# Big 128-column products split into side-by-side pairs of 64 columns in a three-layer graph network on one core

## The reference, cut to what matters

```python
N, E, D, L = 12500, 400000, 64, 3          # nodes, edges, width, layers; dst is sorted
h = relu(layernorm(x))
for l in range(3):
    def mlp(z): return relu(z @ W1[l] + b1[l]) @ W2[l] + b2[l]
    agg = segment_sum(mlp(h[dst]), src, N)  # row = src, col = dst
    h = mlp(h + agg)
out = x + h @ Wf + bf
```

## Time and profile before

| | |
|---|---|
| median of 3 runs | 2153.08 us (2151.14 to 2156.22) |
| the profiled execution | 2150.84 us, of which the span of the trace is 2149.1 us |
| PE busy in the span | 1983.8 us |
| DVE busy | 1443.7 us |
| ACT busy | 840.0 us |
| POOL busy | 598.2 us |
| mean granted TensorE clock | 0.977 |

### The profile page before, as it was taken

How to read it: one execution, slowest core, us unless ns; L and a number is a source line. 1 busy time by engine, 2 the same in 40 slices (tenths; PEclk the granted TensorE clock), 3 DMA queues, 4 the chain that set the end, 5 groups by cost and what they waited for, 6 DMA issues and landing times.

```text
span 2149.1 us, 42352 instructions
## 1 busy us (share of the span) xinstructions
PE 1983.8 (92%) x16959; PEld 1077.5 (50%) x16959; DVE 1443.7 (67%) x1656; ACT 840.0 (39%) x2196; POOL 598.2 (28%) x273
## 2 busy tenths in 40 slices
PE   4565889999999999999999999999999999999998
PEld 3454545555555555544455455455445555555554
DVE  7999999999999999946643343343465444444343
ACT  4896988888888888822200000000010000000000
POOL 3666666666666666600000000000000000000000
PEclk9786999999999999999999999999999999999999
DMA  7356666666666666653444543543544555545452
GB/s 201 73 138 184 176 183 203 200 196 195 192 194 192 193 192 189 187 180 91 151 150 121 164 149 105 171 144 118 164 150 123 171 167 155 161 151 166 137 164 71
DMA packets 332835, 344.60 MB, mean 160 GB/s; under 512 B 21562, under 2 KB 303992, under 8 KB 332184
## 3 DMA queue, kind: packets, MB, share of 16 engines
q1 hardware_dynamic: 327516, 335.59, 53.2%
q0 software_dynamic: 2352, 6.43, 1.1%
q10 hardware_dynamic: 2816, 0.53, 0.2%
HBM read 252.58 MB, written 89.89 MB: 159 GB/s over the span
## 4 chain that ended last, share of the span: by engine, by line
PE 61%; DVE 24%; issue 6%; DMA 4%; POOL 2%; SPq 1%; ACT 1%; DVEq 0%; POOLq 0%
PE ps L1546 49%; DVE arena L756 13%; PE ps L1411 7%; DVE arena L764 5%; DMA arena<-counts_dram 4%; POOL arena L638 2%; PE ps L1496 2%; DVE arena L804 2%; DVE arena L796 2%; PE ps L1378 1%; PE ps L1523 1%; SPq L455 1%; PE ps L1406 1%; DVE arena L729 1%; DMA counts_dram<-arena 1%
## 5 line engine op out<-in xcount | busy, mean ns | idle before, releaser
L1546 PE MATMUL ps<-arena,parts 128*128 128x448 fp8e4 x5488 | 1049.4, 353 | 1.4 <-DVE arena L892 1.4
L1546 PEld LDWEIGHTS ps<-arena,parts 128*128 128x128 f16 x5488 | 531.6, 98 | 518.4 <-issue 27.1
L879 DVE TENSOR_SCALAR arena<-arena 128x3136 uint16<-128x3136 uint16 x196 | 191.3, 976 | 586.8 <-PE ps L1546 586.8
L638 POOL TENSOR_TENSOR arena<-arena,weight_now 128x416 int32<-128x416 int32 x196 | 507.1, 2587 | 279.9 <-DVE arena L756 275.9
L1411 PE MATMUL ps<-arena,parts 128*128 128x448 fp8e4 x2744 | 554.2, 354 | 1.6 <-DVE parts L845 1.6
L756 DVE TENSOR_TENSOR arena<-row_iota,key_now 128x3712 f16<-128x3712 f16 (+1 forms) x196 | 414.5, 2115 | 0.0
L1277 ACT ACTIVATE arena<-arena 128x448 f32<-128x448 f32 x42 | 24.2, 577 | 980.5 <-DVE arena L906 980.5
L1411 PEld LDWEIGHTS ps<-arena,parts 128*128 128x128 f16 x2744 | 255.5, 98 | 279.5 <-issue 57.6
L1184 ACT ACTIVATE arena<-ps 128x800 uint16<-128x800 f32 x392 | 340.3, 879 | 25.4 <-PE ps L1378 25.2
L1378 PE MATMUL ps<-arena 128*128 128x53 fp8e4 x6272 | 205.0, 189 | 108.0 <-POOL arena L638 104.6
L1378 PEld LDWEIGHTS ps<-arena 128*128 128x128 f16 x6272 | 192.1, 98 | 170.1 <-DVE arena L756 83.4
(11 more groups left out here) (150 smaller groups left out, 1048.5 us busy)
## 6 DMA issues: line engine op xcount, KB each, us to landing
arena<-counts_dram SPq DMA_DIRECT2D x294, 784.0 KB, 4.6
counts_dram<-arena SPq DMA_DIRECT2D x784, 100.0 KB, 2.3
h_dram<-parts SPq DMA_DIRECT2D x2, 1536.0 KB, 7.1
edges_dram<-arena SPq DMA_DIRECT2D x2, 1400.0 KB
arena<-in_x_dram SPq DMA_DIRECT2D x14, 192.0 KB
out_dram<-arena SPq DMA_DIRECT2D x14, 192.0 KB
arena<-in_dst_dram SPq DMA_DIRECT2D x1, 1400.0 KB
arena<-in_src_dram SPq DMA_DIRECT2D x1, 1400.0 KB
```

The source lines that it names most:

```text
L638: nc.gpsimd.tensor_tensor(pairs, pairs, weight_now[:, h * HW:(h + 1) * HW].unsqueeze(2).to_broadcast([P, HW, WORDS // 2]), ALU.mult).then_ ...
L879: v.tensor_scalar(spread[:, c % WIDE, 0, :].bitcast(U16), packed, 0x0F0F, None, ALU.bitwise_and)
L1546: last = t.matmul(ps[:, b, 0:NB], parts[:, c * CK + k, :], spread[:, c % WIDE, b // 2, at:at + NB].bitcast(F8), start=start, stop=stop)
```

## The change

Every big product of 128 columns becomes two pairs of products of 64 columns. In a pair both have the same 64 stationary columns; one takes the low nibbles (even nodes) as moving operand and writes partitions 0 to 63, the other the high nibbles (odd nodes) into partitions 64 to 127 of the same bank. The first pair has the upper parts as weights and the second the lower parts, and both add into the same sum. So upper and lower are added in PSUM, and a stretch has two banks in place of four.

```diff
-SBB = 4
-SBC = NB * SBB
+SBB = 2
+SBC = NB * SBB * 2
...
+            def multiply_tile(tile, wide, k, b, exchange, start, stop):
+
+
+                at = k * SBH + b * NB
+                for part in range(2):
+                    for c in range(2):
+                        last = t.matmul(ps[half(c), b, 0:NB], parts[:, tile, half(part)],
+                                        spread[:, wide, c ^ exchange, at:at + NB].bitcast(F8), start=start and part == 0,
+                                        stop=stop and part == 1)
+                return last
...
-                        last = t.matmul(ps[:, b, 0:NB], parts[:, c * CK + k, :],
-                                        spread[:, c % WIDE, b // 2, at:at + NB].bitcast(F8), start=start, stop=stop)
+                        last = multiply_tile(c * CK + k, c % WIDE, k, b, b ^ swapped(l, b), start, stop)
```

What follows from two banks: `read_sums` reads two banks, `keep_sums` keeps two, `add_kept` is called once in a unit, and the two steps `u0` and `u1` become one step `u` of four products of 64 rows by 64 columns:

```diff
-                    wait_alone(pe, s["sums_read"], g * SBB + 2 * b + 2)
-                    for w in range(2):
-                        cols = slice((2 * w + b) * NB, (2 * w + b + 1) * NB)
-                        last = t.matmul(ps[half(w ^ swapped(l, b)), 4 + b, 0:NB], W1s[:, l, :], zP[:, cols], start=True, stop=True)
-                    last.then_inc(s["u_done"], 1)
+                    wait_alone(pe, s["sums_read"], (g + 1) * SBB)
+                    for b in range(SBB):
+                        for r in range(2):
+                            last = t.matmul(ps[half(r ^ b), 4 + b, 0:NB], W1s[half(r), l, :], zP[half(r), b * NB:(b + 1) * NB],
+                                            start=True, stop=True)
+                        last.then_inc(s["u_done"], 1)
```

A bank now needs both nibbles, so the unpacking in the build stage moves, and its waits change:

```diff
-                if u:
-                    dve.wait_ge(s["sums_done"], SBB * (u - 1) + 2)
+                if u and c == 0:
+                    dve.wait_ge(s["chunks_multiplied"], u)
+                elif u:
+                    dve.wait_ge(s["sums_done"], SBB * u)
...
                 if h == 0 and u >= 0:
+                    unpack_high(ROUND * u)
                     unpack_low(ROUND * u + 1)
                 if h == 1 and u >= 0:
-                    unpack_high(ROUND * u)
-                if h == 2 and u >= 0:
                     unpack_high(ROUND * u + 1)
```

In the startup, `nodes` is made on DVE by doubling instead of by POOL's iota, four `node_steps` instead of one stand ahead of the wait for `firsts_shifted`, the two casts of POOL (L612) go to ACT behind the first and the third group of `count_fans`, and `find_starts` is called for group 0 and then once for groups 1 to 6:

```diff
-            nc.gpsimd.iota(nodes, pattern=[[4 * P, KG], [2, P]], base=0, channel_multiplier=0,
-                           allow_small_or_imprecise_dtypes=True).then_inc(s["nodes_made"], 1)
...
-            for half in range(2):
-                c = slice(half * FAN // 2, (half + 1) * FAN // 2)
-                pool.wait_ge(s["columns_cut"], half + 1)
-                nc.gpsimd.tensor_copy(pk_column[:, c, :], by_units(e5)[:, c, :]).then_inc(s["columns_kept"], 1)
...
+                if n in CAST_AT:
+                    half = CAST_AT.index(n)
+                    c = slice(half * FAN // 2, (half + 1) * FAN // 2)
+                    act.wait_ge(s["columns_cut"], half + 1)
+                    a.copy(pk_column[:, c, :], by_units(e5)[:, c, :]).then_inc(s["columns_kept"], 1)
```

More of the change, by code:

```diff
@@ L675, in _ @@
             v = nc.vector
+            v.memset(rises[:, FAN:FAN + 1], float(FAN))
+            link(v.memset(nodes[:, 0:1], 0.0), dve)
+            done = 1
+            while done < P:
+                link(v.tensor_scalar(nodes[:, done:2 * done], nodes[:, 0:done], 2.0 * done, None, ALU.add), dve)
+                done *= 2
+            for k in range(1, KG):
+                last = v.tensor_scalar(nodes[:, k * P:(k + 1) * P], nodes[:, 0:P], 4.0 * P * k, None, ALU.add)
+            link(last, dve)
             dve.wait_ge(s["dst_loaded"], 32)
             v.tensor_copy(firsts, by_units(dst_t)[:, :, 0]).then_inc(s["firsts_made"], 1)
-            dve.wait_ge(s["nodes_made"], 1)
-            link(v.memset(rises[:, FAN:FAN + 1], float(FAN)), dve)
             dve.wait_ge(s["firsts_made"], 1)
@@ L719, in find_starts @@
                 v.tensor_scalar(start_i[:, t], start_f[:, t], float(LAST_START), None, ALU.min).then_inc(s["starts_found"], 1)
-            for n in range(3):
-                find_starts(n)
+            find_starts(range(0, 1))
             less, var, inv, tmp = (stat[:, j, :] for j in range(4))
@@ L740, in _ @@
             v.tensor_tensor(less, counted[:, 1, 0, :], counted[:, 1, 1, :], ALU.add)
-            for n in range(5, GROUPS):
-                find_starts(n)
+            find_starts(range(1, GROUPS))
             dve.wait_ge(s["root_made"], 1)
@@ L1398, in make_message, with add_kept @@
                 last.then_inc(s["message0_done"], 1)
-            def add_kept(u, b, bank):
-                for c in range(2):
+            def add_kept(u):
+                for b in range(SBB):
                     for r in range(2):
-                        rows, to = slice(r * D, (r + 1) * D), slice((r ^ c) * D, (r ^ c) * D + D)
-                        t.matmul(ps[to, bank + c, 0:NB], ident[rows, rows], kept_sums(u % SB, b + c)[rows], start=True, stop=False)
-            def multiply_chunk(u, c, b, bank, stop):
+                        t.matmul(ps[half(r ^ b), b, 0:NB], ident[half(r), half(r)], kept_sums(u % SB, b)[half(r)], start=True,
+                                 stop=False)
@@ L1409, in multiply_chunk @@
+            def multiply_chunk(u, c, b):
                 for k in range(CK):
-                    at = k * SBH + b % 2 * NB
-                    last = t.matmul(ps[:, bank, 0:NB], parts[:, (ROUND * (u // SB) + c) * CK + k, :],
-                                    spread[:, c, b // 2, at:at + NB].bitcast(F8), start=(u < SB or u >= UNITS - SB) and c == 0 and k == 0,
-                                    stop=stop and k == CK - 1)
-                return last
-            def add_bank(u, b):
-                if b == 0:
+                    last = multiply_tile((ROUND * (u // SB) + c) * CK + k, c, k, b, exchanged(u, b),
+                                         (u < SB or u >= UNITS - SB) and c == 0 and k == 0, c == ROUND - 1 and k == CK - 1)
+                return last
@@ L1419, in add_bank @@
+            def add_bank(u, h):
+                c, b = h // SBB, h % SBB
+                if h == 0:
                     pe.wait_ge(s["parts_made"], ROUND * (u // SB + 1))
-                if u >= SB and b % 2 == 0:
-                    pe.wait_ge(s["sums_kept"], SBB * u + b)
-                    add_kept(u, b, 0)
-                elif SBB * u + b >= 2:
-                    pe.wait_ge(s["sums_kept"], SBB * u + b - 1)
-                else:
-                    pe.wait_ge(s["hidden0_kept"], BLOCKS)
@@ L1427, in add_bank @@
-                for c in range(ROUND):
-                    pe.wait_ge(s["low_unpacked" if b < 2 else "counts_unpacked"], ROUND * u + c + 1)
-                    last = multiply_chunk(u, c, b, b % 2, c == ROUND - 1)
-                last.then_inc(s["sums_done"], 1)
+                    if u:
+                        pe.wait_ge(s["sums_kept"], SBB * u)
+                    else:
+                        pe.wait_ge(s["hidden0_kept"], BLOCKS)
+                    if u >= SB:
+                        add_kept(u)
@@ L1432, in turn_weights @@
+                pe.wait_ge(s["counts_unpacked"], ROUND * u + c + 1)
+                last = multiply_chunk(u, c, b)
+                if c == ROUND - 1:
+                    last.then_inc(s["sums_done"], 1)
+                elif b == SBB - 1:
+                    last.then_inc(s["chunks_multiplied"], 1)
             def turn_weights():
@@ L1559, in _ @@
                 i = u - (UNITS - SB)
-                banks = range(SBB) if i < 0 else BANKS
                 for c in range(ROUND):
```

100 lines of the change are left out of this document (45 added, 55 removed).

## The result

The changed kernel takes 2221.07 us (median of 4 runs, 2220.51 to 2223.81). The kernel before takes 2153.95 on the same chip (4 runs, 2151.14 to 2156.22). The ratio is 1.0319, with a 95% interval of 1.0303 to 1.0335. The forecast was 2129 us and faster; it came out 67 us slower, 92 us above the forecast and outside the range.

A forecast was written before the change was run, and what follows sets the result against it. DVE was taken to bound the build stage, PE layers 1 and 2, DVE and ACT the startup. Terms -14.0 - 4.5 - 0.9 + 0.5 + 0.5 - 5.6 = -24.0 us gave 2129 us, range 2116 to 2168.

The forecast's parts named there:

- The pair: Big products on PE: two 64-column products run side by side at the old product's cost, 0 ns extra, 3 ns upper side.
- B: Rival, chance 0.20: each pair costs a few ns more, from issue or slower weight loads; no gain left at 4.0 ns.
- C: Rival, chance 0.12: pairs do not run side by side at full rate; about 2440 us or more, or about 3570 us.
- The stops: Layers 1 and 2: `u0` and `u1` become one step, one stop fewer in each of 14 stretches, 14 x 1.0 = -14.0 us.
- The build stage: 215 to 918 us: DVE keeps its work and the new `unpack_low` wait is covered; +0.5 us, bounds 0 and +4.
- the last units: Six of the last units: `u0` and `u1` become one step, 0.75 us less each, -4.5 us.
- Rival D: Build stage, chance 0.06: the new `unpack_low` wait binds, DVE stands about 1 us in 40 tile pairs, +40 us, 2169 us.
- The startup: Before the build stage: no iota wait, casts on ACT, fewer `find_starts`; reciprocal 5.6 us earlier, bounds -3 and -7.
- Rival E: Startup gives little because ACT becomes its bound, 2132 us; chance not separate, part of the forecast's range.
- The end: Very end: DVE adds both halves of U after the single `u`, where one was done earlier; +0.5 us.
- PE remains busy through layers 1 and 2 with the clock at 1.00: Expected sign in the profile after: in layers 1 and 2 PE stays busy throughout at full granted clock.
- the rival on the other side: Rival B, chance 0.20: a charge on each pair, which makes the kernel slower from 4.0 ns on.

The follow-up runs named there:

- a_hint: The changed kernel with a prefetch hint for the back-edge at the top of each pass of PE's two loops; 2129.72 us, ratio 0.9898 to before.
- a_unroll: The changed kernel with PE's loops over the stretches of layers 1 and 2 written out; 2131.60 us, ratio 0.9901 to before.
- b_unroll: The kernel before with PE's loops over the stretches written out in the same way; 2151.92 us, ratio 1.0003 to before.

## Why the prediction was wrong

**The pair: as forecast.** Zero extra was taken, 189.6 ns; it is 189.8 in the changed kernel's chain (224 pairs in 42.51 us) and 189.6 in that of `a_hint` (252 in 47.79). Two 64-column products at full rate do run side by side, and rivals B and C, the two that held a third of the chances, are out. Also their weight loads hide: one of 64 columns takes 111 ns (the L1424 load row) where one of 128 took 98, beside matmuls all the time, and nothing is added to the distance. The Trainium skill's rule (TensorE: Matmul & The Clock Gate, Part 3) that a load overlaps only when the row group differs does not hold for these pairs either, which all use the same rows; the same Part also lets a load run ahead into a background weight buffer, which would fit.

**The stops: as forecast.** A stretch with no slow branch takes 77.68 us in layer 1 and 76.65 in layer 2 in `a_unroll` and `a_hint`, against 78.62 and 77.61 before: 0.95 less, where 1.0 was said.

**The build stage: as forecast, within its spread.** Layer 1 begins at 1032.1 against 1042.0, 9.9 us earlier; -5.6 - 4.5 - 0.9 + 0.5 gives -10.5. The same build code ends elsewhere in each execution: layer 1 begins at 1035.6 in `a_unroll` and at 1030.4 in `a_hint`, so one trace fixes this term to some 3 us and no better. In the last units the step from one to the next falls from 14.81 to 14.12 us, 0.69 where 0.75 was said. Rival D is out: in DVE's groups between 215 and 918 us, `unpack_low` waits for a transfer as before, and for PE only 0.6 us (2.5 in `a_unroll`), where D asked for 40:

```profile
L806 DVE TENSOR_SCALAR arena<-arena 128x3136 uint16<-128x3136 uint16 x78 | 74.6, 957 | 10.5 <-DMA arena<-counts_dram 9.7 <-PE ps L1424 0.6
```

**The startup: as forecast.** -6.3 for -5.6 at the reciprocal; the two operations at 2.2 us are back at 0.99, and POOL's casts are gone. Rival E is out.

**The end: slightly under.** From the end of the last big product to the end of the span it takes 13.3 us against 12.3, +1.0 for +0.5:

```profile
2206.46 0.98 PE L1508 MATMUL ps<-arena,W1s 64*64 64x448 f32 x8 [0.78 <-DVE arena L902]
2209.37 0.75 PE L1536 MATMUL ps<-Wfb,arena 64*64 64x64 f32 x28 [1.92 <-ACT arena L1287]
```

**The step that failed** is "PE remains busy through layers 1 and 2 with the clock at 1.00", and behind it the sum's own premise that a product costs only its distance to the next. The sum had no term for the program of the loop: twice the products are twice the loads and matmuls, so the body goes from 977 to 1753 records. "Twice as many instructions" stood in the prediction, but only as a charge on each pair, never as a size that the sequencer must hold. No rival had this mechanism, and the rival on the other side was a different one. The price, by row: from the first product of layer 1 to the W1 products of the last stretch it takes 1174.4 us (1032.1 to 2206.5), against 1082.4 in `a_unroll` (1035.6 to 2118.0), 92 us more. Ten passes that follow a taken back-edge make 90.3 of them: 10.3 to 11.0 us each in layer 1, 6.5 to 8.1 in layer 2. Of the 90.3, 58.0 are PE's idle time, and the other 32 follow from the clock: after a stop the next pairs run at the lower level, 0.373 us apart instead of 0.190. The last 1.7 us are 56 products at the lower clock where layer 1 begins, with no back-edge ahead of them. Forecast 2129 plus 92 is 2221, measured 2221; that it fits so closely is in part luck, since without the stops the change gives 20 to 22 us and not the 24.0 of the sum, and before took 2151.84 us beside those runs, not 2153.08.

Could it be seen ahead? The sequencer's line of the loop was in the trace of before, with 0.22 us for each branch, and no instruction packet at all between 1200 and 1590 us: the body was held, so a body of another size was an untested case. It was also countable, since the changed kernel's text gives its instructions. The price of not being held stood in no row, and from the trace of before no bound could be made for it. It should have stood as a rival of unknown price.

## What to carry to other kernels

When a change multiplies the instructions inside an engine's loop, count them for one pass and compare with the largest body whose branch is known to be short; that the products cost the same per column tells nothing of it. In a trace the sign is idle time released by "issue" once in a pass, together with branches of microseconds in the sequencer and packets in the instruction queue while the loop repeats; a body that is held shows none. The cure costs one line, either the hint on the back-edge or the loop written out, and it should be tried before the change itself is given up: here it turned 1.032 into 0.990. The hint is not free: it left a stop of 1.8 us at one loop's end, and it did not hold a body of 1953 records.

## What the runs showed of the hardware that was not expected

- Without the hint, a taken branch of PE's loop cost 0.21 to 0.24 us with bodies of 960 to 1529 records, and 6.2 to 6.7 us with 1736 to 1952. No size between was run. Straight code of the same length had no such stop (`a_unroll`, `b_unroll`), though `a_unroll` fetched nearly as many packets as the changed kernel:

```profile
q8 instruction: 198, 3.24, 0.7%
```

- A stop of 5 us costs more than itself. In layer 1 the granted clock over the next 10.8 us was 0.58. In layer 2 the 56 products behind the first back-edge took 8.37 us (6.8 to 8.4 over the five), where the chain has 5.42 at 1.00:

```profile
1784.67 1.30 PE L1424 MATMUL ps<-arena,parts 128*64 128x448 fp8e4 x12
1790.94 8.37 PE L1424 MATMUL ps<-arena,parts 128*64 128x448 fp8e4 x56 [4.97 <-issue]
```

- The hint on the back-edge took 31 ns and made 6.6 us into 0.22 by leaving the body where it was: 1754 and 1918 records were not fetched again. 1953 were, and PE then stood 1.6 to 1.7 us behind each branch.
- In layer 1 a second wait of 1.45 to 1.6 us stands 2.45 us behind the first one, and in layer 2 of the same kernel there is none. A packet of instructions starts in the 2.45 us between the two (at 1284.09 us in the chain above, 1.1 us long), so the second wait looks like one for the next block of code; why layer 2 has none was not found.
